# Transposing attention probabilities on VectorE instead of TensorE, inside a fused attention and MLP block

## What is computed

```python
h = film(rmsnorm(x, norm1_w), cond, film1_w, film1_b)   # x * (1 + scale) + shift, per sequence
Q = h @ q_w + q_b; K = h @ k_w + k_b; V = h @ v_w + v_b
scores = jnp.einsum('bnd,bmd->bnm', Q, K) * D ** (-0.5)
attn = jax.nn.softmax(scores, axis=-1)
out = jnp.einsum('bnm,bmd->bnd', attn, V)
x = x + (out @ proj_w + proj_b)
h = film(rmsnorm(x, norm2_w), cond, film2_w, film2_b)
return x + gelu(h @ mlp_w1 + mlp_b1) @ mlp_w2 + mlp_b2  # hidden size 2048
```

## Time and profile before

| what | us |
|---|---|
| median of the timed runs | 1755.91 |
| profiled execution | 1755.86 |
| its span | 1754.1 |
| TensorE matmuls busy | 1746.5 (100%) |
| VectorE busy | 1268.4 (72%) |
| ScalarE busy | 890.5 (51%) |
| GpSimd busy | 196.0 (11%) |

### The profile page before, as it was taken

The page is one execution under the profiler, slowest core; times in us unless marked ns, Lnnn a source line. Parts: engine busy times, 40 slices in busy tenths (PEclk is TensorE's granted clock), DMA queues, the critical chain, the costliest instruction groups (busy, mean ns, idle before and its releaser), DMA issues.

```text
span 1754.1 us, 23184 instructions
## 1 busy us (share of the span) xinstructions
PE 1746.5 (100%) x8310; PEld 1467.6 (84%) x8310; DVE 1268.4 (72%) x1743; ACT 890.5 (51%) x1498; POOL 196.0 (11%) x202
## 2 busy tenths in 40 slices
PE   9999999999999999999999999999999999999999
PEld 7888888888888888888888888888888888888887
DVE  5878888556665887588588768858866885885477
ACT  6645445545554554455465445546544554653344
POOL 0467676000000000000000000000000000000000
PEclk9999999999999999999999999999999999999999
DMA  9577787732237678668867876876787787677676
GB/s 330 166 269 289 251 300 277 262 101 88 79 120 216 192 261 272 201 219 269 243 190 265 269 202 220 271 243 190 264 267 203 224 269 239 192 240 245 194 228 203
DMA packets 202323, 395.83 MB, mean 226 GB/s; under 512 B 24161, under 2 KB 28257, under 8 KB 200161
## 3 DMA queue, kind: packets, MB, share of 16 engines
q1 hardware_dynamic: 202208, 394.34, 69.2%
HBM read 331.25 MB, written 62.98 MB: 225 GB/s over the span
## 4 chain that ended last, share of the span: by engine, by line
PE 93%; DMA 3%; DVE 1%; POOL 1%; ACT 1%; SPq 0%; issue 0%; POOLq 0%; DVEq 0%
PE psum L703 35%; PE psum L723 23%; PE psum L591 12%; PE psum L731 12%; PE psum L631 3%; PE psum L632 3%; PE psum L673 3%; PE psum L636 3%; DMA x_tok<-x_dram 1%; DMA wd_scratch<-w_out 1%; POOL w_out L561 1%; DMA rs_scratch<-rstd 0%; DVE h L1099 0%; PE psum L605 0%; PE psum L664 0%
## 5 line engine op out<-in xcount | busy, mean ns | idle before, releaser
L703 PE MATMUL psum<-op_hi_P,ring 128*128 128x512 f32 x1792 | 552.0, 389 | 0.0
L723 PE MATMUL psum<-stage_hi,ring 128*128 128x512 f32 x1784 | 440.6, 389 | 0.0
L703 PEld LDWEIGHTS psum<-op_hi_P,ring 128*128 128x128 f32 x1792 | 336.2, 188 | 69.6
L723 PEld LDWEIGHTS psum<-stage_hi,ring 128*128 128x128 f32 x1784 | 334.9, 188 | 69.4
L938 ACT CAST stage_hi<-x 128x1024 fp32r<-128x1024 f32 x224 | 235.4, 1054 | 235.2 <-PE psum L723 223.0
L703 PE MATMUL psum<-op_lo_P,ring 128*128 128x512 f32 x896 | 348.6, 389 | 0.0
L1316 DVE TENSOR_TENSOR stage_lo<-x,stage_hi 128x1024 fp32r<-128x1024 f32 x224 | 273.5, 1224 | 72.4 <-ACT stage_hi L938 72.1
L922 ACT ACTIVATE x<-x,vecs 128x512 f32<-128x512 f32 x192 | 138.1, 723 | 283.9 <-DVE x L1303 283.8
L731 PE MATMUL psum<-stage_lo,ring 128*128 128x512 f32 x892 | 238.4, 389 | 0.0
L703 PEld LDWEIGHTS psum<-op_lo_P,ring 128*128 128x128 f32 x896 | 168.2, 188 | 34.8
L731 PEld LDWEIGHTS psum<-stage_lo,ring 128*128 128x128 f32 x892 | 167.5, 188 | 34.7
(11 more groups left out here) (168 smaller groups left out, 2244.5 us busy)
## 6 DMA issues: line engine op xcount, KB each, us to landing
ring<-wu_scratch SPq DMA_DIRECT2D x448, 256.0 KB, 3.0
ring<-wd_scratch SPq DMA_DIRECT2D x448, 256.0 KB, 2.9
x_tok<-x_dram SPq DMA_DIRECT2D x16, 1024.0 KB, 9.7
xT_in<-xT_dram SPq DMA_DIRECT2D x16, 1024.0 KB, 8.8
x2T_scratch<-xT_in SPq DMA_DIRECT2D x32, 512.0 KB, 3.6
hn<-x2T_scratch SPq DMA_DIRECT2D x32, 512.0 KB, 5.4
xres<-x2T_scratch SPq DMA_DIRECT2D x32, 512.0 KB, 4.5
out_dram<-xres SPq DMA_DIRECT2D x31, 512.0 KB, 4.4
```

The costliest lines, as they stand in the source:

```text
L703: mm = pe.matmul(to, wt, b, start=q in FRESH and t == 0, stop=t == len(steps) - 1, skip_group_check=True)
L723: mm = pe.matmul(bank(q, dt), a[:, dt, part, :], stage_hi[r][:, e, :], start=q in FRESH and ss == 0 and e == 0 and part == 0, stop=False, ...
```

## The change

The probabilities are transposed by VectorE: sixteen operations per group, each on a 32x32 block position of all four sequences, from `probs` straight into `pT_sb`. TensorE's four transposes and ScalarE's copy are gone. TensorE takes g blocks 0 and 1 of the next group together, by passes (high x high and low x high for both blocks, then high x low), ahead of outputs 0 and 1, and block 2 where block 1 was. ScalarE casts the high halves ahead of the exponentials, and VectorE makes the low halves ahead of the reciprocal. In the start, the first two norm rows go through GpSimd's DMA queue, and SP issues its loads without waiting for them; ScalarE's film coefficients come behind all weight casts; there are 9 warm-up products instead of 11. In groups 8 and 9 three loads change places.

The diff, cut to its core (semaphores that are only merged are left out):

```diff
-WARM_UP = 11
+WARM_UP = 9
...
             def load_norm1_row(m):
-                sp.wait_ge(rstd_stored, 16 * m + 16)
+                sp.wait_ge(rstd_stored, 16 * (m - 1))
...
                 if k == 2:
                     load_xT(0)
-                    norm1_to_row(0)
-                if k == KD - 1:
-                    load_norm1_row(0)
...
-                if n == CHUNKS:
-                    load_hn(0)
-                    sp.dma_start(f2w_sb[:], ...)
...
                 if n + 4 <= LAST:
                     load_x_tok(n + 4)
+                if n == CHUNKS:
+                    load_hn(0)
+                if n == CHUNKS + 1:
+                    sp.dma_start(f2w_sb[:], ...)
...
-            for m in range(3):
+            for m in range(2):
                 norm1(m)
+                pool.wait_ge(rstd_done, m + 1)
+                nc.gpsimd.dma_start(rs[m].rearrange("(p j) -> p j", p=P), rstd[:]).then_inc(first_rstd_stored, 16)
+                pool.wait_ge(first_rstd_stored, 16 * m + 16)
+                nc.gpsimd.dma_start(norm1_row[m][:], rs[m:m + 1, :].broadcast_to([P, TOK])
+                                     ).then_inc(first_row_loaded, 16)
+            norm1(2)
...
+            def g_pair(m):
+                p = m % 2
+                pe.wait_ge(h_hi_done, GB * m + GB)
+                for j in range(2):
+                    pe.wait_ge(v_read, GB * (m - 1) + j + 1)
+                    for k in range(KD):
+                        pe.matmul(gv[j], qk_hi[:, k, tokens(j)], h_hi[p][:, k, :], start=k == 0, stop=False)
+                        pe.matmul(gv[j], qk_lo[:, k, tokens(j)], h_hi[p][:, k, :], start=False, stop=False)
+                pe.wait_ge(h_lo_done, GB * m + GB)
+                for j in range(2):
+                    for k in range(KD):
+                        mm = pe.matmul(gv[j], qk_hi[:, k, tokens(j)], h_lo[p][:, k, :], start=False, stop=k == KD - 1)
+                    mm.then_inc(g_full, 1)
...
                 if n > 0:
-                    g_product(n, 2)
                     g_product(n, 3)
...
-                transpose_probs(n)
                 if n < LAST:
-                    g_product(n + 1, 0)
+                    g_pair(n + 1)
...
                 if n < LAST:
-                    g_product(n + 1, 1)
+                    g_product(n + 1, 2)
...
-                if k == 1:
-                    film1_coefs()
+            film1_coefs()
...
+                if n < LAST:
+                    for k in range(KD):
+                        h_high(n + 1, k)
                 act.wait_ge(bias_done, n + 1)
                 for b in range(GB):
                     nc.scalar.activation(probs[:, b, :], score_b[:, b, :], ACT.Exp, ...)
-                if n < LAST:
-                    for k in range(KD):
-                        h_high(n + 1, k)
...
-                act.wait_ge(pT_full, n + 1)
-                nc.scalar.copy(pT_sb[:], pT).then_inc(pT_read, 1)
...
+            def transpose_probs(n):
+                dve.wait_ge(probs_scaled, n + 1)
+                wait_used(dve, out_full, GB * n)
+                for i in range(0, P, 32):
+                    for j in range(0, P, 32):
+                        last = dve.transpose(pT_sb[j:j + 32, :, i:i + 32], probs[i:i + 32, :, j:j + 32])
+                last.then_inc(pT_done, 1)
...
+                if n < LAST:
+                    wait_used(dve, v_full, GB * n)
+                    for k in range(KD):
+                        h_low(n + 1, k)
                 dve.wait_ge(exp_done, GB * n + GB)
                 dve.reciprocal(rden[:], den[:]).then_inc(rden_done, 1)
...
+                transpose_probs(n)
                 if n < LAST:
-                    wait_used(dve, v_full, GB * n)
-                    for k in range(KD):
-                        h_low(n + 1, k)
                     key_terms(n + 1)
```

More of the change, by code:

```diff
@@ L247, in cond_block_kernel @@
         wk_loaded, wq_loaded, wpT_loaded = (sem(n) for n in ("wk_loaded", "wq_loaded", "wpT_loaded"))
-        wk_bq_done, wq_bk_done, wp_bv_done, attn_col_done = (
-            sem(n) for n in ("wk_bq_done", "wq_bk_done", "wp_bv_done", "attn_col_done"))
+        bias_cols_done = sem("bias_cols_done")
+        first_rstd_stored, first_row_loaded = sem("first_rstd_stored"), sem("first_row_loaded")
         one_plus_done, film1_bias_done, bq_bk_done = (sem(n) for n in ("one_plus_done", "film1_bias_done", "bq_bk_done"))
@@ L262, in cond_block_kernel @@
             sem(n) for n in ("g_full", "g_read", "v_full", "v_read", "scored", "top_done", "bias_done", "exp_done"))
-        rden_done, probs_scaled, pT_full, pT_read, out_full, out_read = (
-            sem(n) for n in ("rden_done", "probs_scaled", "pT_full", "pT_read", "out_full", "out_read"))
+        rden_done, probs_scaled, pT_done, out_full, out_read = (
+            sem(n) for n in ("rden_done", "probs_scaled", "pT_done", "out_full", "out_read"))
         w_src_loaded, w_mixed, w_hi, w_split = (sem(n) for n in ("w_src_loaded", "w_mixed", "w_hi", "w_split"))
@@ L521, in norm1 @@
                 pool.wait_ge(summed, GB * m + GB)
-                wait_used(pool, rstd_stored, 16 * m)
+                if m > 2:
+                    pool.wait_ge(rstd_stored, 16 * (m - 2))
                 nc.gpsimd.tensor_tensor(rstd[:], sumsq[:], eps_sum[:].broadcast_to([P, GB]),
@@ L648, in key_row @@
                 pe.wait_ge(key_lo_done, n + 1)
-                wait_used(pe, pT_read, n)
-                product(pT, [(ones_r[:], key_hi[:]), (ones_r[:], key_lo[:])], key_row_full)
+                wait_used(pe, key_col_done, GB * n)
+                product(key_ps, [(ones_r[:], key_hi[:]), (ones_r[:], key_lo[:])], key_row_full)
             def scores(n):
@@ L658, in scores @@
                             scored if b == GB - 1 else None)
[L660 to L665, removed]
             def output(n, d):
                 if d == 0:
-                    pe.wait_ge(pT_read, n + 1)
+                    pe.wait_ge(pT_done, n + 1)
                     pe.wait_ge(v_read, GB * n + GB)
@@ L961, in _ @@
             sum_squares(1)
-            act.wait_ge(wk_bq_done, KD)
+            act.wait_ge(bias_cols_done, KD)
             for j in range(KD - 1):
@@ L1096, in scale_x @@
                 dve.wait_ge(xT_loaded[m % 3], 16 * (m // 3) + 16)
-                dve.wait_ge(row_loaded[m % 2], 16 * (m // 2) + 16)
+                if m < 2:
+                    dve.wait_ge(first_row_loaded, 16 * m + 16)
+                else:
+                    dve.wait_ge(row_loaded[m % 2], 16 * (m // 2))
                 for k in range(KD):
@@ L1199, in operand_low, with bias_column @@
                                   ALU.subtract).then_inc(op_lo_done, 1)
-            def bias_column(w_sb, bias_sb, into, loaded_sem, done):
+            def bias_column(w_sb, bias_sb, into, loaded_sem):
                 dve.wait_ge(loaded_sem, 32)
@@ L1205, in bias_column @@
                     dve.tensor_tensor_reduce(w_sb[:, k, :], w_sb[:, k, :], bias_sb[:], 1.0, 0.0, ALU.mult, ALU.add,
-                                             into[:, k:k + 1]).then_inc(done, 1)
+                                             into[:, k:k + 1]).then_inc(bias_cols_done, 1)
             for k in range(KD):
@@ L1231, in _ @@
                 vp_low(c)
[L1232 to L1233 removed]
+            bias_column(wk_sb, bq_row, wk_bq, wk_loaded)
+            bias_column(wq_sb, bk_row, wq_bk, wq_loaded)
             dve.wait_ge(bq_bk_done, 1)
[L1235 removed]
+            dve.wait_ge(bias_cols_done, 2 * KD)
             key_terms(0)
             key_low(0)
[L1238 to L1240 removed]
+            bias_column(wpT_sb, bv_row, attn_col, wpT_loaded)
+            dve.wait_ge(bias_cols_done, 3 * KD)
+            dve.tensor_tensor(attn_col[:], attn_col[:], col("bp"), ALU.add).then_inc(bias_cols_done, 1)
             for n in range(GROUPS):
```

26 lines of the change are left out of this document (9 added, 17 removed).

## The result

The changed kernel takes 1776.6 us (median of 4 runs, 1773.7 to 1777.5) against 1755.6 beside it: ratio 1.0115, interval 1.0102 to 1.0127. It is slower, as forecast (1765.6), and inside the range (1746 to 1783), but the loss is 21 us where 9.7 were forecast, more than twice as much. The profiled execution took 1775.83, with a span of 1774.0, 19.9 more than before.

A forecast was written before the change was run, and what follows sets the result against it. TensorE's own matmuls were taken to bound the kernel. From 1755.86 us, 7.0 for its transposes and 1.7 for the start came off, and 18.4 of stalls were added: 1765.6 us, range 1746 to 1783.

The forecast's parts named there:

- The mechanism: Attention groups: VectorE's loop with sixteen transposes outlasts TensorE's 29.43 us, so TensorE stalls before the first output.
- the unstalled group: A group in which TensorE never waits: 29.87 less 0.44 us for the removed transposes, 29.43 us.
- group 1: Its stall before the first output: 1.1 us, as GpSimd starts about 2 us sooner for it.
- the last group: TensorE's wait there for the transposes, ready at 523.1 against 523.8: 0.7 us, taken as 1.0.
- the stalls: TensorE's waits before first outputs: 16.3 us in groups 2 to 8, 1.1 in group 1, 1.0 in the last; 18.4 together.
- the size of the loop in groups 2 to 8: VectorE's loop between first outputs: 31.8 us against TensorE's 29.43, a stall of 2.33 us in each of seven groups.
- the term of the low halves: VectorE's low halves ahead of the reciprocal, partly beside GpSimd: 3.4 us, bounds 2.49 (no contention) and 5.0 (all of it).
- To the third output's addition: First stretch of the loop, from a group's first output to VectorE adding the third: 5.45 us.
- From there to the bias: VectorE's gapless work from the third output's addition to the exponentials' bias: 16.53 us, as before the change.
- The bias: VectorE's short operation for the exponentials: 0.16 us plus 0.8 waiting for GpSimd's running operation.
- The transposes: Sixteen VectorE transposes at 0.28 us each without overlap: 4.5 us, bounds 3.4 and 9.8.
- The start: Norm row through GpSimd's queue lands at 28.2, g products start at 36.8 instead of 38.5: -1.7 us.

The follow-up runs named there:

- The kernel with filler: The changed kernel with ten more matmuls on TensorE in groups 1 to 8, in the stall before the outputs and overwritten by them: 1772.6 us, ratio 1.0087.
- the exchanged loops: The changed kernel with the transposes' two loops swapped, so four in a row write the same 32 partitions but read four different ones: 1775.8 us, ratio 1.0109.
- the transposes in place: The changed kernel with each transpose reading and writing the same 32 partitions, blocks not exchanged, so the attention's result differs: 1759.1 us, ratio 1.0013.

## Why the prediction was right in kind and half in size

**The mechanism held.** TensorE waits for VectorE's transposes ahead of the first output, in the groups forecast (1 to 8 and the last) and not in 9 to 14. Undoing the transposes, moving GpSimd or shortening its work each took the wait away in groups 2 to 8. The terms for the unstalled group (29.43, measured 29.40), for group 1 and for the last group came out within 0.25 us. One agreement is luck: the stalls were forecast at 18.4 us together, and TensorE's waits add up to 18.4. The idle of a group is up to 2.75 us, not 2.33; three idles are shorter since slow outputs came before them; and the stalls cost 25.3 us, not 18.4.

**The step that failed is the size of the loop in groups 2 to 8,** 31.8 us forecast, 32.43 to 33.01 measured, and in it above all the term of the low halves, 3.4 us forecast and 5.0 measured. For the group of 32.43 that begins at 101.91:
- To the third output's addition 5.75, not 5.45: behind the stall the outputs begin with 2.05 us, not 1.78, and VectorE waits for the third.
- From there to the bias 15.2, not the 16.53 of before. Scaling and modulation took 4.78 and 4.40 us, not 5.04 and 4.84, and the low half of the key row 0.79, not 1.43, from start to start.
- The bias cost 0.44, not 0.96. That VectorE waits out GpSimd's running operation held: the maximum's addition ends at 122.83, GpSimd's subtraction at 122.81; the bias ends at 123.39, GpSimd's cast at 123.36. But casts of 0.61 us stand between the operations of 1.3 us that the 0.8 was taken from, and the bias met one of them.
- By these the low halves began 1.6 us sooner than reckoned, 21.4 after the transposes, and GpSimd ended later, at 25.96 instead of 24.9, since its own operations are slower where the two meet (1.6 us against 1.3). So they lay nearly wholly beside it: 5.0 us, the upper bound, where I took 3.4 from a partial overlap. What VectorE had gained by arriving 1.6 us sooner it lost again on them.
- The transposes took 5.1 with TensorE's start behind them, not 4.5 and 0.1. I had the row of 0.28 us for one operation, and a transpose is 0.303, spaced 0.317.

With 0.1 for reciprocal and scaling these are +0.3 - 1.3 - 0.5 + 1.6 + 0.1 + 0.5 = +0.7 per group. Seven groups make 4.9 of the 6.5 us that this row of the account is short.

**What the prediction didn't have at all was the clock:** 1.6 us in groups 2 to 8 and 1.6 of the 1.9 in group 9. A stall was priced as its idle time. The kernel with filler shows 3.1 us of this to be the granted clock. It could not be read from the trace before the change, whose one large wait is of 2.1 us with a clock of 1.00 behind it.

**The start** was wrong too, -1.7 forecast and +1.5 measured. The norm row was to land at 28.2, by a load of 4.0 us from 24.2 on. The store did land sooner (21.93, before 24.20), but the load took 6.53 us (before 4.63), now beside the loads of weights: 425 GB/s moved from 24 to 27 us, where it had been 81. That the one comes of the other is likely, but no run separates them. And TensorE's products were put at an end of about 36, though before the change they end 9.5 us after the row (28.94 to 38.48): with the row at 28.2 that is 37.7, a gain of 0.7 and not 1.7. Besides, whoever reads the earlier trace rows once takes for a constant what moves by 2 us and more between executions. "What sets it" could be shown (the low halves behind the scaling); "what the new queue is worth" could not.

**The loads of group 8** were called worth nothing to TensorE. Two more of TensorE's waits before the change, both in group 9, are that cost (1.2 us in all):

```profile
PE psum L631 <- ACT h_hi L870: 0.5, 1, 0.5
PE psum L664 <- DVE probs L1275: 0.3, 1, 0.3
```

**The whole difference** of 10.3 us between the account's columns is then 4.9 for the loop, 1.6 for the clock inside groups 2 to 8, 1.9 for group 9 (1.6 of clock, and outputs of 2.05 us in place of 1.78 behind group 8's stall), 3.2 for the start and 0.4 for groups 1 and 15, less 1.2 for the loads and 0.5 for the transposes.

**The rules weighed.** The traces settle the one on held instructions. A transpose of 32 partitions by 128 elements whose blocks change partitions waits for the one before it: 303 ns long, 317 apart. Kept on one block of partitions, sixteen take 3.58 us. The Trainium skill, VectorE: DVE Perf Modes, section Two Vector instructions with no wait between them, has it so, for outputs and for the first input alike, and the exchanged loops bear out the input's part. Its 311 ns in The three transpose paths is given for bf16 128x128, and that it is near 303 is no more than that: a full-width instruction of 128x512 took 711 ns here. By the rule and 0.317 us a transpose my sum would have been 0.6 us per group higher, 4 us, and still short by the low halves and the clock.

## What to carry to other kernels

When work leaves the bound engine for one with room on average, close the loop on the receiving engine for one period, and give each of its operations the price that it has at its new place beside the shared neighbour. An operation that comes sooner can meet a neighbour that it used to miss; start the neighbour by an event that puts it beside operations that don't suffer, before giving up the move. Price a stall of the bound engine above its idle time: look for idles of its length in any trace of the kernel, and for the granted clock behind them.

## What the runs showed of the hardware

- VectorE's 32x128 fp32 transposes are not slowed by GpSimd (5.05 us for sixteen with and without), while subtractions, key terms and scalings of 128x512 double (0.61 to 1.26 us).
- GpSimd is slowed as well: 1.6 us for a subtraction beside VectorE's two-input operations, 1.3 otherwise.
- Small VectorE operations (128x4) beside GpSimd ended with the operation that it had running: 122.83 with 122.81 and 123.39 with 123.36 us in one group, 155.83 with 155.81 in the next. With GpSimd idle they take 0.16 us.
- Idles of TensorE and its clock, in the waits for the transposes of three kernels (changed, 11 warm-up products, loops exchanged): of twelve idles of 2.74 to 2.79 us eleven were followed by a stretch partly at 1.2 GHz, of fourteen of 1.24 to 1.59 us none, and the one of 1.84 us was. Nor did the clock fall behind the seven of 1.1 to 1.3 us with the transposes in place, or the seven that were filled down to 0.3 to 0.5. Why the one of 2.74 was spared and the one of 1.84 not is open.
- Sixteen 32-partition transposes cost 5.05 us, one of all 128 partitions with the same elements 0.71.
